# Attention's divisions by the softmax sums on GpSimd instead of VectorE, from the sixth group on

## The reference

```python
x = x + cross(ctx, ctx, layernorm(x), mask)   # 16 heads of 16: softmax(q k / 16) v, then Wo
x = x + self_attn(layernorm(x))               # 16 heads: softmax over the 64 largest scores of each row
```

## Time and profile before

| | us |
|---|---|
| median of 3 runs | 1491.79 (1490.87 to 1492.78) |
| profiled execution, its time | 1491.98 |
| profiled execution, span of its trace | 1490.5 |
| DVE busy | 1202.7 (81%) |
| ACT busy | 1020.2 (68%) |
| POOL busy | 438.0 (29%) |

### The profile page before, as it was taken

How to read it: one execution, slowest core, us unless ns; L and a number is a source line. 1 busy time by engine, 2 the same in 40 slices (tenths; PEclk the granted TensorE clock), 3 DMA queues, 4 the chain that set the end, 5 groups by cost and what they waited for, 6 DMA issues and landing times. The chain is left out here.

```text
span 1490.5 us, 31867 instructions
## 1 busy us (share of the span) xinstructions
PE 1300.1 (87%) x11808; PEld 803.6 (54%) x11808; DVE 1202.7 (81%) x3761; ACT 1020.2 (68%) x1673; POOL 438.0 (29%) x392
## 2 busy tenths in 40 slices
PE   7999899999999998999977799778979879677746
PEld 4555556655566665666644586466447437333213
DVE  1253249999999999999999999998886687787882
ACT  5878778888788887788863554476787678644521
POOL 4111012222323223222222322312443443542550
PEclk9999999999999999999988999889989989787867
DMA  7878411333033203312105123115556356223320
GB/s 152 193 182 269 114 23 37 58 58 58 3 58 58 35 26 59 58 16 44 44 2 189 57 71 99 58 44 148 143 160 172 105 146 184 79 78 100 109 61 8
DMA packets 96857, 132.70 MB, mean 89 GB/s; under 512 B 20192, under 2 KB 80872, under 8 KB 93744
## 3 DMA queue, kind: packets, MB, share of 16 engines
q1 hardware_dynamic: 96688, 130.50, 35.0%
HBM read 124.95 MB, written 5.51 MB: 88 GB/s over the span
## 5 line engine op out<-in xcount | busy, mean ns | idle before, releaser
L1478 ACT ACTIVATE attn_arena<-ps 128x1024 f32<-128x1024 f32 x512 | 497.6, 1025 | 131.4 <-PE ps L478 127.9
L2135 DVE MATCH_REPLACE8 attn_late<-attn_shared,attn_late 128x256 f32<-128x256 f32 x1024 | 412.0, 411 | 0.0
L2132 DVE MAX8 attn_shared<-attn_late 128x8 f32<-128x256 f32 x1024 | 381.7, 415 | 15.1 <-ACT attn_late L1504 12.6
L478 PE MATMUL ps<-attn_arena 32*128 32x256 f32 x4096 | 344.6, 404 | 8.5 <-ACT attn_arena L1478 4.2
L478 PEld LDWEIGHTS ps<-attn_arena 32*128 32x128 f32 x4096 | 232.5, 186 | 94.5 <-issue 64.6
L492 PE MATMUL ps<-attn_arena 128*32 128x256 f32 x4096 | 277.3, 387 | 4.3 <-ACT attn_early L1486 3.1
L1357 POOL TENSOR_SCALAR attn_late<-attn_late 128x512 f32<-128x512 f32 x64 | 95.7, 1495 | 539.0 <-DVE attn_late L2135 538.9
L492 PEld LDWEIGHTS ps<-attn_arena 128*32 128x32 f32 x4096 | 108.5, 109 | 135.2 <-issue 59.3
L764 PE MATMUL ps<-attn_arena,attn_q 128*128 128x512 f32 x256 | 130.0, 640 | 13.9 <-ACT attn_arena L1574 7.6
L1370 POOL TENSOR_TENSOR attn_late<-attn_late 128x1024 f32<-128x1024 f32 x48 | 113.0, 2360 | 93.4 <-DVE ps L1976 93.4
L786 PE MATMUL ps<-attn_arena 128*128 128x256 f32 x512 | 126.7, 393 | 0.0
(11 more groups left out here) (273 smaller groups left out, 1651.8 us busy)
## 6 DMA issues: line engine op xcount, KB each, us to landing
attn_arena<-ctxT SPq DMA_DIRECT2D x124, 256.0 KB, 4.8
attn_arena<-ctx SPq DMA_DIRECT2D x32, 512.0 KB, 4.2
attn_late<-rows SPq DMA_DIRECT2D x256, 64.0 KB, 2.3
attn_arena<-ctxV SPq DMA_DIRECT2D x15, 1024.0 KB, 13.1
attn_late<-maskT SPq DMA_DIRECT2D x20, 512.0 KB, 6.9
attn_late<-wide SPq DMA_DIRECT2D x64, 128.0 KB, 2.8
attn_early<-wide SPq DMA_DIRECT2D x64, 128.0 KB, 3.3
attn_arena<-maskT SPq DMA_DIRECT2D x12, 512.0 KB, 11.8
```

Source lines behind the costliest of these rows:

```text
L478: mm = pe.matmul(ps[:, first + j - 2 * i, u * S:(u + 1) * S], kx[n % 2][rows, k0:k0 + P], qpad[rows, n % GROUPS, b * S:(b + 1) * S], start ...
L1478: act.activation(probs[m % 2][:, 2 * i:2 * i + 2], ps[:, first:first + 2, :], ACT.Exp, scale=1.0 / 16.0).then_inc(exp_done, 1)
L2132: dve.max(top[:, t, turn], s[:, i, t] if turn == 0 else work[:, i, t]).then_inc(picked, 1)
L2135: dve.match_replace(work[:, i, t], top[:, t, turn], s[:, i, t] if turn == 0 else work[:, i, t], LOW).then_inc(picked, 1)
```

## The change

For the eleven groups 5 to 15 (`pool_divides`), ACT copies both halves of the turned sums out of `M_` into a new tile `turned` in SBUF (`copy_turned`): in slot 0 of round `p + 1` for the first three groups of a batch, and in slot 2 of round `p`, behind `soft`, for the last. The copy releases the bank. GpSimd then runs the new `divide`, behind `keep_top`: a power of -1 of the 8 sums a partition, a product of 128 elements, a power of the 8 sums of the self half, and two products of 64 elements, each waiting for the one before. Groups 0 to 4 stay on DVE, in a `divide` that has lost its second half. In batches 1 to 3 `check` moves from turn 5 to turn 6 and waits for GpSimd's division. `find_bad` stands behind the division on GpSimd.

```diff
--- before.py
+++ after.py
@@ -158,6 +158,15 @@
     return (group // GROUPS, group % GROUPS) if 0 <= group < BESIDE // HG else None
 
 
+def pool_divides(n):
+    return self_group(n) is not None
+
+
+def turned_groups(p):
+    n = (p - FIRST_P) // CROSS_PER - 1
+    return [n] if (p - FIRST_P) % CROSS_PER == 0 and 0 <= n < B * GROUPS else []
+
+
 def due(name, p, slot):
     return [b for b in range(B) if DUE[name][b] == (p, slot)]
 
@@ -287,6 +296,7 @@
         mzero = sb("mzero", [P, B, MASK_PIECES])
         mfold = sb("mfold", [P, 8])
         accT = cut(early, 0, 2, 2, S)
+        turned = cut(early, 3072, 2, S)
         recip = cut(shared, 704, T, H)
         chk = cut(shared, 736, T * H)
         least = sb("least", [P, 1])
@@ -1359,6 +1369,26 @@
                 pool.wait_ge(e_ready, T * (p + 1))
                 pool.tensor_tensor(pm[:], pm[:], e[:, i], ALU.mult).then_inc(pm_ready, 1)
 
+            def divide(n):
+                b, g = n // GROUPS, n % GROUPS
+                pool.wait_ge(misc_taken, misc["acc", b, g] + 1)
+                cross = turned[:, 0].rearrange("p (t j v) -> p t j v", t=T, j=HG)
+                mine = recip[:, :, g * HG:(g + 1) * HG]
+                step(pool.tensor_tensor(mine, cross[:, :, :, D], gone_m[:], ALU.pow))
+                step(pool.tensor_tensor(heads[:, :, g * HG * D:(g + 1) * HG * D].rearrange("p t (j d) -> p t j d", d=D), cross[:, :, :, 0:D],
+                                        mine.unsqueeze(3).to_broadcast([P, T, HG, D]), ALU.mult))
+                sb, sg = self_group(n)
+                own = turned[:, 1].rearrange("p (t j v) -> p t j v", t=T, j=HG)
+                step(pool.tensor_tensor(srecip[:], own[:, :, :, D], gone_m[:], ALU.pow))
+                part = ao[:, :, sg * HG * D:(sg + 1) * HG * D].rearrange("p t (i n) -> p t i n", i=2)
+                for t in range(T):
+                    half = part[:, t] if t == 0 else part[:, t, ::-1]
+                    ins = pool.tensor_tensor(half.rearrange("p i (j d) -> p i j d", d=D), own[:, t, :, 0:D].rearrange("p (i j) d -> p i j d", i=2),
+                                             srecip[:, t].rearrange("p (i j) -> p i j", i=2).unsqueeze(3).to_broadcast([P, 2, HG // 2, D]), ALU.mult)
+                    if t < T - 1:
+                        step(ins)
+                ins.then_inc(ao_ready, 1)
+
             def weigh_states(i, half):
                 n = i * N_HALF + half
                 if n < FIRST_DRIVEN:
@@ -1407,6 +1437,12 @@
                     root(INTRO[p - FIRST_P + 1])
                 if 0 <= p - 1 < B * H:
                     keep_top(p - 1)
+                for n in turned_groups(p - 1):
+                    if pool_divides(n) and n % GROUPS < GROUPS - 1:
+                        divide(n)
+                for n in turned_groups(p):
+                    if pool_divides(n) and n % GROUPS == GROUPS - 1:
+                        divide(n)
                 if ending and d == 0:
                     branch["pool", h] = pool.mark_branch_hint_location()
                     find_bad(h)
@@ -1586,6 +1622,11 @@
                     act.wait_ge(c_pv, n - 1)
                 act.copy(cpT[:, n % 2], c_bank(n)).then_inc(c_pT, 1)
 
+            def copy_turned(n):
+                act.wait_ge(misc_made, misc["acc", n // GROUPS, n % GROUPS] + 1)
+                act.wait_ge(ao_ready, n - FIRST_BESIDE)
+                act.copy(turned.rearrange("p i s -> p (i s)"), M_).then_inc(misc_taken, 1)
+
             def soften(i):
                 d = i % 2
                 act.wait_ge(cv_ready, i + 1)
@@ -1700,6 +1741,9 @@
                     soft(p)
                 if slot == 3 and BESIDE <= done < B * H:
                     take_sums(done)
+                for n in (turned_groups(p - 1) if slot == 0 else turned_groups(p) if slot == 2 else []):
+                    if pool_divides(n) and slot == (2 if n % GROUPS == GROUPS - 1 else 0):
+                        copy_turned(n)
                 row_duties(p, slot)
 
             act.wait_ge(first_made, 1)
@@ -1843,25 +1887,15 @@
                 dve.wait_ge(misc_made, misc["acc", b, g] + 1)
                 turned = M_[:, 0:S].rearrange("p (t j v) -> p t j v", t=T, j=HG)
                 step(dve.reciprocal(recip[:, :, g * HG:(g + 1) * HG], turned[:, :, :, D]))
-                last = dve.tensor_tensor(heads[:, :, g * HG * D:(g + 1) * HG * D].rearrange("p t (j d) -> p t j d", d=D), turned[:, :, :, 0:D],
+                ins = dve.tensor_tensor(heads[:, :, g * HG * D:(g + 1) * HG * D].rearrange("p t (j d) -> p t j d", d=D), turned[:, :, :, 0:D],
                                          recip[:, :, g * HG:(g + 1) * HG].unsqueeze(3).to_broadcast([P, T, HG, D]), ALU.mult)
-                if self_group(GROUPS * b + g):
-                    sb, sg = self_group(GROUPS * b + g)
-                    turned = M_[:, S:2 * S].rearrange("p (t j v) -> p t j v", t=T, j=HG)
-                    step(dve.reciprocal(srecip[:], turned[:, :, :, D]))
-                    part = ao[:, :, sg * HG * D:(sg + 1) * HG * D].rearrange("p t (i n) -> p t i n", i=2)
-                    for t in range(T):
-                        half = part[:, t] if t == 0 else part[:, t, ::-1]
-                        last = dve.tensor_tensor(half.rearrange("p i (j d) -> p i j d", d=D), turned[:, t, :, 0:D].rearrange("p (i j) d -> p i j d", i=2),
-                                                 srecip[:, t].rearrange("p (i j) -> p i j", i=2).unsqueeze(3).to_broadcast([P, 2, HG // 2, D]), ALU.mult)
-                    last.then_inc(ao_ready, 1)
-                    dve.wait_ge(ao_ready, GROUPS * sb + sg + 1)
-                    dve.sem_inc(misc_taken, 1)
-                else:
-                    last.then_inc(misc_taken, 1)
+                ins.then_inc(misc_taken, 1)
+                dve.wait_ge(misc_taken, misc["acc", b, g] + 1)
 
             def check(b):
                 r = recip[:].rearrange("p t h -> p (t h)")
+                if b:
+                    dve.wait_ge(ao_ready, GROUPS * (b + 1) - FIRST_BESIDE)
                 step(dve.tensor_scalar(chk[:], r, SMALLEST, None, ALU.is_ge))
                 step(dve.scalar_tensor_tensor(out=chk[:], in0=r, scalar=LARGEST, in1=chk[:], op0=ALU.is_le, op1=ALU.mult))
                 dve.tensor_reduce(least[:], chk[:], AX.X, ALU.min).then_inc(checked, 1)
@@ -2043,7 +2077,7 @@
                     for i in passes(5, p):
                         gate_pass(i)
                     n = (p - 1 - FIRST_P) // CROSS_PER - 1
-                    if (p - 1 - FIRST_P) % CROSS_PER == 0 and 0 <= n < B * GROUPS and n % GROUPS < GROUPS - 1:
+                    if (p - 1 - FIRST_P) % CROSS_PER == 0 and 0 <= n < B * GROUPS and n % GROUPS < GROUPS - 1 and not pool_divides(n):
                         divide(n // GROUPS, n % GROUPS)
                     if p - 1 >= 0 and (p - 1) // H < B and (p - 1) % H == 0:
                         add_v((p - 1) // H)
@@ -2106,8 +2140,9 @@
                     for i in passes(-2, p):
                         add_log(i)
                 if turn == 5 and ending and d == 0:
-                    divide(h, GROUPS - 1)
-                    dve.wait_ge(misc_taken, misc["acc", h, GROUPS - 1] + 1)
+                    if h == 0:
+                        divide(h, GROUPS - 1)
+                if turn == (5 if h == 0 else 6) and ending and d == 0:
                     check(h)
                 if turn == 0 and ending and d == 2:
                     dve.wait_ge(bo0_added, h + 1)
```

## The result

| | before | after |
|---|---|---|
| median of 9 runs each | 1492.18 (1489.99 to 1495.17) | 1500.75 (1495.04 to 1506.04) |
| ratio after / before | | 1.0044, 95% interval 1.0025 to 1.0063 |
| profiled execution, time (span) | 1491.98 (1490.5) | 1495.04 (1493.3) |
| two more executions profiled, span | | 1504.5, 1498.5 |

The kernel is slower, as forecast: 8.6 us by the medians, where I had forecast 11.0 (1502.8). Two later comparisons of the same two kernels gave 1.0066 (1.0053 to 1.0079) and 1.0055 (1.0035 to 1.0075). The profiled execution of after is the fastest of its nine, so its span must not be set against the median: I use all three profiles of after where sizes matter.

The account below looks back on a forecast made before the run. DVE and PE were taken to bound the kernel by turns. Endings losing 17.1 us less 6.1 gained in other rounds gave 11.0, added to 1491.8: 1502.8 us, range 1489.5 to 1508.5.

Parts of the forecast that it names:

- part 3: Last group's division in rounds 13, 29 and 45 delays `count_bad` and the joints: 6.5 + 6.5 + 4.1 = 17.1 us lost.
- cheap power: Rival: GpSimd's power of 8 elements costs what 2 do; endings lose 8.1, net +2.0 us, 1494 to 1497; 24%.
- The power's price: GpSimd's power of 8 elements in each division: 0.73 or 2.27 us, upper taken, making a division 5.9 us.
- my two laws: The power's extra 0.52 us over a plain operation is paid once (0.73 for 8 elements) or per element (2.27).
- the 6.8 goes through, less the 0.3: First two endings: `count_bad` 6.8 us later reaches the joint, less PE's 0.3 idle behind it, since PE comes last.
- Part 1: Divisions leaving DVE in the ordinary rounds: gains of 2.3, 1.4 and 2.4 us reach the three joints, together 6.1.
- price not in the sum: PE's wait at `count_bad` may lower its clock: 0 to 3 us in each of the first two endings, taken as 0.
- Part 2: ScalarE's eight slot 0 copies cost 0 (bound 2.4 us); GpSimd's work, 10.6 in a round of 11.5, fits at cost 0.
- Faster: Rival: the endings' delay doesn't reach the joint, GpSimd done before about 371; gain 9.6 to 12.9 us, 1479 to 1482; 14%.
- Low clock: Rival: as forecast, and PE falls to 1.2 GHz for several us in two endings; +14 to +17, 1506 to 1509; 12%.
- port lock: Rival: DVE stands still during GpSimd's 5.9 us divisions, eleven times; 65 us on top; 2%.

Follow-up runs that it names:

- e1_last_on_dve: The change with groups 7, 11 and 15 divided on DVE again and checked at turn 5: 1488.58 us, 0.9974 of before; run again 1487.98, 0.9965.
- e2_only_last_on_pool: The kernel before with only groups 7, 11 and 15 divided on GpSimd, the other eight left on DVE: 1506.07 us, 1.0093 of before.
- e6_copies_added: The kernel before with eight extra ScalarE copies of 128x512 in slot 0 that nothing reads: 1491.85 us against 1491.62, ratio 1.0006.
- e3_early_copy: The change with ScalarE's copy of the last group moved ahead of slot 2's exponentials: 1490.51 us, 0.9979 of before.
- filled kernels: The change with eight, or six, unread PE matmuls ahead of PE's wait for the flag: 1501.57 us, 1.0066 of before; with six 1498.48, 1.0033.

## Why the prediction was right, and where its sizes were off

**Direction and mechanism.** Slower, because the division of the last group stands in the chain of an ending and GpSimd takes four times as long for it as DVE: this was the forecast's part 3, and `e1_last_on_dve` (undone: 12 us faster than after) and `e2_only_last_on_pool` (alone: 13.6 slower than before) show it from both sides. The range from 1489.5 to 1508.5 holds the measured 1500.75; its low end was not worked out soundly, since the cheap power's 8.1 us of loss would have to be met by a gain of 10.4, more than the eight divisions are worth (9.4).

**The power's price** was open between 0.73 and 2.27 us; I took the upper end. It is 1.65. With 0.714 for 2 elements that is 0.157 an element and 0.40 once, if the exponent (-0.5 there, -1 here) makes no difference: neither of my two laws, but something between. The division is 4.6 instead of 5.9, inside the range of 2.9 to 5.9. Put into the forecast, each ending is 1.25 cheaper and the sum 7.25.

**The chain of an ending, step by step.** The copy starts as the exponentials end and takes 0.59, GpSimd starts 0.1 later, and 1.6 us pass from the end of the division to `count_bad` (371.21 to 372.84): all as worked out. DVE waited 5.1, 5.2 and 2.3 at `check`, forecast 6.2 in the first and about 6 and 4: less by the cheaper division. `count_bad` starts 5.7 us later against the joint in after (372.84 - 192.9 = 179.9) than in `e1_last_on_dve` (174.2), where I had 6.8, or 5.55 with the measured division. By the last table the three endings come 5.7, 5.8 and 3.4 later in after than in the two `e1` profiles (forecast 6.8, 6.8 and 4.4; with the measured division 5.55, 5.55 and 3.15), and 5.7, 5.5 and 1.6 later in `e2_only_last_on_pool` than in before and `e6_copies_added`.

**The step that did not hold: "the 6.8 goes through, less the 0.3".** From `count_bad` to the joint I took PE's 17.4 us as fixed. They aren't: the stall behind the branch shrinks when `count_bad` is late, and the clock moves. The means from `count_bad` to the joint are 16.8, 15.5 and 16.9 us in before and `e6_copies_added`, 17.7, 15.8 and 15.8 in after, 19.9, 16.3 and 17.2 in the two `e1` profiles. Against before the stall given back and the time lost to the clock about cancel (+0.8, +0.3, -1.1): the 3.5, 3.8 and 0.9 us by which after is behind at `count_bad`, 8.3 in all, arrive at the joints as 8.2. Against the two `e1` profiles, whose first ending ran at the low clock, the endings cost only 3.3, 5.1 and 2.0 from joint to joint; `e2_only_last_on_pool` less before gives 5.2, 6.4 and 0.6. The forecast was 6.5, 6.5 and 4.1. In the third ending PE's timeline shows the stall at work. Before, with 4.46 of stall, then after, where the stall is gone and `count_bad` had waited instead:

```profile
783.06 1.12 PE L599 MATMUL ps<-ident,attn_early 128*128 128x128 f32 x4 [4.46 <-issue]
```

```profile
782.65 0.59 PE L551 MATMUL ps<-attn_bad,attn_ones 128*128 128x1 f32 x2 [5.78 <-POOL attn_bad L1273]
784.34 1.11 PE L609 MATMUL ps<-ident,attn_early 128*128 128x128 f32 x4 [1.10 <-ACT attn_general L1526]
787.59 1.11 PE L669 MATMUL ps<-ident,attn_late 128*128 128x128 f32 x4 [2.14 <-POOL attn_late L1370]
```

Counted from the joint ahead of them, `count_bad` comes 0.8 us later than before (188.8 against 188.0), `turn_heads` 2.6 earlier (190.5 against 193.1). Little of that reaches the end: PE now waits 1.10 us for the flag's copy and 2.14 for the selected weights. In the second profile of after the stall of 4.3 was there again, and that third part took 204.8, against 203.8 and 204.6 without it.

**Part 1's gain.** 6.1 forecast; 3.9 and 5.8 by the medians of the two comparisons of `e1_last_on_dve`. At `count_bad` it is 2.2, 2.0 and about 2.5 us, against 2.3, 1.4 and 2.4. By the parts from joint to joint (before's means 193.2, 201.2, 204.6 less the `e1` means 194.2, 200.2, 202.4) it is -1.0, 1.0 and 2.2: the first was made and lost again behind the first branch, where the clock fell to 0.81. That loss stands in the "price not in the sum"; I had looked for it behind a longer wait of PE only, and it also came without one. From the side of `e2_only_last_on_pool` the first part's gain is 0.9. That the forecast of after's first part agrees to 0.1 is therefore luck of two errors: from joint to joint the gain was 1.4 to 3.3 smaller than forecast and the ending 1.3 to 3.2 cheaper, and the mean itself is no better than 1 to 2 us.

**Part 2.** ScalarE's copies at 0 (bound 2.4): measured 0 to 1. GpSimd's round fits: up to round 13 PE's waits behind `keep_top` got shorter (3.0 us in seven waits before, 0.5 in two after). The one behind the third branch grew, from 0.50 to 2.14 us, because PE gets there sooner without the stall. DVE's waits at 476 and 667, forecast to grow by 1.2 each, are 1.44 (was 1.22) and 2.02 (was 1.35); but what DVE saved is lost beside them, in waits of 0.63 at 464, 0.24 at 500, 0.43 at 656 and 0.29 at 707 that before did not have, so the sums grew by 1.1 and 1.4, as forecast.

**Rivals.** "Faster" named its own condition, a copy ahead of the exponentials, and 1479 to 1482 for it. `e3_early_copy` is that kernel and gave 1490.5: the sign is right, the size isn't: the division still takes 4.6, DVE still waits 0.8 to 1.0 us for it at the check, and the gain of the first part doesn't arrive (193.2 to the joint, as before). Low clock: it came. PE's busy time behind `count_bad` is 0.5 us longer than before's own in the first ending in two profiles of after and 2.9 in one, and 1.4 to 2.9 longer in the second. The port lock did not. DVE's timeline in round 6, beside GpSimd's power from 279.70 to 281.37:

```profile
278.14 0.75 DVE L2167 MAX8 attn_shared<-attn_late 128x8 f32<-128x256 f32 x2
...
279.58 0.75 DVE L2167 MAX8 attn_shared<-attn_late 128x8 f32<-128x256 f32 x2
...
281.02 0.75 DVE L2167 MAX8 attn_shared<-attn_late 128x8 f32<-128x256 f32 x2
```

```profile
279.70 1.67 POOL L1377 TENSOR_TENSOR attn_shared<-attn_early,attn_gone_m 128x8 f32<-128x8 f32 x1
```

The turn is 1.44 us beside the power and 1.44 with GpSimd idle (286.78 to 288.22), so MAX8 and MATCH_REPLACE8 aren't held up. That is no contradiction of the lock in the Trainium skill (SBUF — State Buffer, section "Who interferes with whom"), which names operations with two SBUF inputs or in a 2-port mode, and lets whichever instruction was issued first keep the ports. Beside GpSimd's divisions DVE ran only MAX8, MATCH_VALUE_LOAD and MATCH_REPLACE8. The rows of the last two name two tiles each, but the eight values are loaded by the first of them and MATCH_REPLACE8's shape is of the scores alone; taken so, no operation of the rule's kinds ran there, and the rule itself was not tried.

**What stays open.** Why the stall behind the branch is there in some executions and not in others of the same kernel (the page lists a DMA queue of kind "instruction", so late loading of PE's instructions is a candidate, which no run tried and nothing in the traces joins to these stalls); why the clock fell in `e1_last_on_dve` and not in `e6_copies_added` at the same place; how much of the loss the low clock is; and the 4 us behind the last joint in the filled kernels. A version that beats both kernels, if by little, is `e1_last_on_dve`: 0.9974 and 0.9965 of before, some 12 us below after.

## What to carry to other kernels

Taking an operation off a busy engine pays where it stands between others, and costs where its result is waited for: split the change by that, and move only the first kind (here eight of eleven). For a link of a chain the price is the new engine's latency with its queue, not the busy time saved, and a copy in front of it inherits all that stands ahead of it in its engine's list; that place alone was some 10 us here. And a delay at one wait need not add to the next stall of the same engine but can overlap it, so look what idles right behind before taking a delay as passed on.

## What the runs showed of the hardware

- GpSimd's power: 0.71 us for 128x2 (of -0.5), 1.65 for 128x8 (of -1); a product 0.29 for 128x64 and 0.40 for 128x128.
- Behind the branch of the first two endings PE stalled 1.2 to 2.9 us with nothing that the profile shows, and 0 to 1.0 where the work just ahead of the branch had come 3.5 us or more late; at the third ending it stalled 4.0 to 6.0 or not at all, whatever the wait. The cause is not shown.
- While PE idled 5.6 us (367.2 to 372.8 us in after) its granted clock fell: it was about 1.00 up to 371 and 0.50, that is 1.2 GHz, from 371 to 377. In a kernel where it multiplied during that time it was 1.00, and the same 147 matmuls took 11.1 instead of 14.5 us.
- A PE matmul of 128x512 takes 0.90 us (six in 5.42, eight in 7.13).
- Executions of the same code differ by up to 5.6 us in the first 195 us: a single profile can't size a change of 0.5%.
